# Attention with float32 probabilities and values in place of float16 high and low parts

## The reference, cut to what matters

```python
qg = split_heads(tokens @ Wqg, HEADS)      # 16 heads
kv = split_heads(tokens @ Wkv, HEADS)
queries, gates = qg[..., :16], qg[..., 16:]
keys, values = kv[..., :16], kv[..., 16:]  # values: 64 wide
queries, keys, values = l2norm(queries), l2norm(keys), l2norm(values)
sim = einsum('bhid,bhjd->bhij', queries, keys)
attn = square(relu(sim))
aggr = einsum('bhij,bhjd->bhid', attn, values)
out = tanh_norm(aggr) * tanh(silu(gates))
return out @ Wout
```

## Time and profile before

| | us |
|---|---|
| time, median of 2 runs | 3120.34 (3120.2 to 3120.49) |
| span of the profiled execution | 3118.2 |
| granted TensorE clock, mean | 0.976 |
| PE busy | 2774.7 (89%) |
| DVE busy | 2549.5 (82%) |
| ACT busy | 2288.4 (73%) |
| POOL busy | 888.1 (28%) |

### The profile page before, as it was taken

One profiled execution on the slowest core, in us unless ns is written; L12 is line 12 of the kernel. 1 busy time (PEld: TensorE's weight loads), 2 busy tenths in 40 slices (PEclk: granted clock), 3 DMA queues, 4 the chain that ended last, 5 costly groups with the idle time before them and its releaser, 6 DMA issues.

```text
span 3118.2 us, 54633 instructions
## 1 busy us (share of the span) xinstructions
PE 2774.7 (89%) x15168; PEld 1174.7 (38%) x15168; DVE 2549.5 (82%) x5207; ACT 2288.4 (73%) x4138; POOL 888.1 (28%) x683
## 2 busy tenths in 40 slices
PE   2898998989989899998989989899898998989999
PEld 1343343333433344333433334333343333434433
DVE  8987879778687887878878788786987879888796
ACT  3787767778677786877868678686776867778686
POOL 0314123141332413224132231412314123141332
PEclk8999999999999999999999999999999999999999
DMA  3000000000000000000000000000000000000000
GB/s 154 7 1 21 1 22 1 1 22 1 22 1 1 22 1 22 1 1 22 1 22 1 1 22 1 22 1 22 1 1 22 1 22 1 1 22 1 14 1 8
DMA packets 19501, 40.23 MB, mean 13 GB/s; under 512 B 1584, under 2 KB 9904, under 8 KB 18128
## 3 DMA queue, kind: packets, MB, share of 16 engines
q1 hardware_dynamic: 19152, 36.11, 3.4%
HBM read 27.72 MB, written 8.39 MB: 12 GB/s over the span
## 4 chain that ended last, share of the span: by engine, by line
PE 40%; DVE 35%; issue 14%; ACT 7%; DVEq 2%; POOL 1%; ACTq 0%; DMA 0%; SPq 0%; POOLq 0%
PE wk L1104 18%; DVE pl L589 10%; PE acc L1104 10%; DVE ph L585 7%; PE av L1177 5%; DVE wide L505 2%; PE sim L1163 2%; ACT ring L899 2%; PE wk L1186 2%; DVE hf L609 2%; DVE vn_t L418 1%; ACT ring L903 1%; ACT sg L909 1%; PE wk L1228 1%; DVE vn_y L420 1%
## 5 line engine op out<-in xcount | busy, mean ns | idle before, releaser
L1056 POOL TENSOR_TENSOR hl<-hf,hh 128x512 f16<-128x512 f32 x288 | 369.5, 1283 | 1645.8 <-ACT hh L915 1482.0
L589 DVE TENSOR_TENSOR pl<-ring,ph 128x512 f16<-128x512 f32 x1024 | 759.9, 782 | 0.0
L899 ACT ACTIVATE ring<-sim 128x512 f32<-128x512 f32 x1024 | 567.5, 603 | 250.3 <-PE sim L1163 176.6
L903 ACT ACTIVATE ring<-ring 128x512 f32<-128x512 f32 x1024 | 593.6, 640 | 0.0
L585 DVE CAST ph<-ring 128x512 f16<-128x512 f32 x1024 | 472.0, 497 | 83.0 <-ACT ring L903 54.3
L1177 PE MATMUL av<-ph,vh 128*64 128x512 f16 x1024 | 211.7, 410 | 42.5 <-DVE pl L589 42.4
L609 DVE SCALAR_TENSOR_TENSOR hf<-wk,up_routed,sg 128x512 f32<-128x512 f32 x256 | 191.6, 749 | 66.9 <-PE wk L1104 16.3
L909 ACT ACTIVATE sg<-wk,inv_m 128x512 f32<-128x512 f32 x288 | 199.6, 693 | 46.6 <-PE wk L1104 46.4
L1077 POOL TENSOR_TENSOR pl<-wide,ph 128x512 f16<-128x512 f32 x128 | 169.6, 1329 | 211.4 <-ACT ph L947 211.4
L641 DVE TENSOR_TENSOR gate_sb<-gate_sb,wk 128x512 f32<-128x512 f32 x128 | 87.8, 686 | 162.9 <-PE wk L1228 162.7
L1104 PE MATMUL acc<-hh,down_h 128*128 128x512 f16 x576 | 220.2, 382 | 0.0
(11 more groups left out here) (192 smaller groups left out, 5386.4 us busy)
## 6 DMA issues: line engine op xcount, KB each, us to landing
x_sb<-x SPq DMA_DIRECT2D x16, 512.0 KB, 4.9
y_sb<-x_t SPq DMA_DIRECT2D x16, 512.0 KB, 4.3
out_t<-y_sb SPq DMA_DIRECT2D x16, 512.0 KB, 3.2
raw_wa<-wa SPq DMA_DIRECT2D x1, 2560.0 KB, 9.1
raw_gate<-w_gate SPq DMA_DIRECT2D x1, 2304.0 KB, 14.2
raw_up<-w_up SPq DMA_DIRECT2D x1, 2304.0 KB, 19.3
raw_down<-w_down SPq DMA_DIRECT2D x1, 2304.0 KB, 24.3
raw_wo<-w_out SPq DMA_DIRECT2D x1, 1024.0 KB, 26.1
```

Source lines behind the costliest of these rows:

```text
L589: v.tensor_tensor(pl[:, n % NH_, :], ring[:, n % NR_, :], ph[:, n % NH_, :], ALU.subtract).then_inc(pl_done, 1)
L899: a(ring[:, n % NR_, :], sim[n % 2][:, :], ACT.Relu, scale=S_SCALE).then_inc(relu_done, 1)
L903: a(ring[:, n % NR_, :], ring[:, n % NR_, :], ACT.Square).then_inc(square_done, 1)
L1056: tt(hl[:, n % 2, :], hf[:, n % 2, :], hh[:, n % 2, :], ALU.subtract).then_inc(h_lo, 1)
```

## The change

The float16 parts of probabilities and values go. A probability stays in the `ring`, now of 8 slots; VectorE computes it as score (from PSUM) times relu (from the ring), and ScalarE's square, VectorE's cast and subtraction and the splits of v on ScalarE and GpSimd are gone. AV is one float32 matmul for each head, with the scaled values `v_raw` as weights and the ring slot as moving operand. As the score bank is now read by the square, S(s) waits for `square_done` where it waited for `relu_done`. `agg` gets a buffer of its own.

```diff
-        NR_, NH_ = 4, 2 * (LAG + 1)
+        NR_, NH_ = 8, 2
...
-        ph, pl = sb("ph", [P, NH_, T], F16), sb("pl", [P, NH_, T], F16)
+        ah, al = sb("ah", [P, NH_, T], F16), sb("al", [P, NH_, T], F16)
...
-        agg = wide
+        agg = sb("agg", [P, NP_, T])
...
-            def probs(b, n):
-                dve.wait_ge(square_done, upto(b, 2 * STEPS, n + 1))
-                dve.wait_ge(av_step, upto(b, STEPS, n // 2 - LAG))
...
-                v.tensor_copy(ph[:, n % NH_, :], ring[:, n % NR_, :]).then_inc(ph_done, 1)
-
-            def probs_lo(b, n):
...
-                v.tensor_tensor(pl[:, n % NH_, :], ring[:, n % NR_, :], ph[:, n % NH_, :],
-                                ALU.subtract).then_inc(pl_done, 1)
+            def square(b, n):
+                dve.wait_ge(relu_done, upto(b, 2 * STEPS, n + 1))
+                v.tensor_tensor(ring[:, n % NR_, :], sim[n % 2][:, :], ring[:, n % NR_, :],
+                                ALU.mult).then_inc(square_done, 1)
...
                     for n in (2 * s, 2 * s + 1):
-                        probs(b, n)
+                        square(b, n)
                     for kind, e in PLAN[s][len(lead):]:
                         expert_item(b, kind, e)
-                    for n in (2 * s, 2 * s + 1):
-                        probs_lo(b, n)
...
-            def split_hi_v(b, n):
...
             def relu(b, n):
                 act.wait_ge(sim_full, upto(b, 2 * STEPS, n + 1))
-                act.wait_ge(pl_done, upto(b, 2 * STEPS, n - NR_ + 1))
-                if n < NR_:
+                act.wait_ge(av_step, upto(b, STEPS, (n - NR_) // 2 + 1))
+                if n < NB:
                     act.wait_ge(qk_lo, upto(b, 2 * NB, 2 * NB))
-                a(ring[:, n % NR_, :], sim[n % 2][:, :], ACT.Relu, scale=S_SCALE).then_inc(relu_done, 1)
-
-            def square(b, n):
-                act.wait_ge(relu_done, upto(b, 2 * STEPS, n + 1))
-                a(ring[:, n % NR_, :], ring[:, n % NR_, :], ACT.Square).then_inc(square_done, 1)
+                a(ring[:, n % NR_, :], sim[n % 2][:, :], ACT.Relu, scale=S_SCALE * S_SCALE).then_inc(relu_done, 1)
...
-            def split_lo_v(b, n):
...
-                    pe.wait_ge(relu_done, upto(b, 2 * STEPS, n - 1))
+                    pe.wait_ge(square_done, upto(b, 2 * STEPS, n - 1))
...
-                pe.wait_ge(pl_done, upto(b, 2 * STEPS, 2 * s + 2))
+                pe.wait_ge(square_done, upto(b, 2 * STEPS, 2 * s + 2))
                 if pair == 0:
-                    pe.wait_ge(v_lo, upto(b, 2 * NB, 2 * (j + 1)))
+                    pe.wait_ge(vn_done, upto(b, 2 * NB, 2 * (j + 1)))
...
-                for i, (vv, pp) in enumerate(((vh, ph), (vl, ph), (vh, pl))):
-                    for half in range(2):
-                        h = 2 * pair + half
-                        ins = mm(av[64 * half:64 * half + 64, :], vv[:, j, h * DV:(h + 1) * DV],
-                                 pp[:, (2 * s + half) % NH_, :], start=(j == 0 and i == 0),
-                                 stop=(j == NB - 1 and i == 2))
+                for half in range(2):
+                    h = 2 * pair + half
+                    ins = mm(av[64 * half:64 * half + 64, :], v_raw[:, j, h * DV:(h + 1) * DV],
+                             ring[:, (2 * s + half) % NR_, :], start=(j == 0), stop=(j == NB - 1))
                 ins.then_inc(av_step, 1)
```

More of the change, by code:

```diff
@@ L209, in build_layer @@
         xh, xl = sb("xh", [P, KD, T], F16), sb("xl", [P, KD, T], F16)
-        NR_, NH_ = 4, 2 * (LAG + 1)
+        NR_, NH_ = 8, 2
         ring = sb("ring", [P, NR_, T])
-        qk_raw = ring[:, :, :]
+        qk_raw = ring[:, 0:NB, :]
         sq = sb("sq", [P, 2, T])
@@ L239, in build_layer @@
         y_sb = sb("y_sb", [P, KD, T])
-        ph, pl = sb("ph", [P, NH_, T], F16), sb("pl", [P, NH_, T], F16)
+        ah, al = sb("ah", [P, NH_, T], F16), sb("al", [P, NH_, T], F16)
         wide = sb("wide", [P, NP_, T])
         v_raw = wide[:, :, :].rearrange("p (k a) t -> p k (a t)", k=NB)
-        agg = wide
+        agg = sb("agg", [P, NP_, T])
         qst, kst = sb("qst", [P, 2, 2 * T], F16), sb("kst", [P, 2, 2 * T], F16)
         qt, kt = sb("qt", [P, NP_, T], F16), sb("kt", [P, NP_, T], F16)
-        vh, vl = sb("vh", [P, NB, H * DV], F16), sb("vl", [P, NB, H * DV], F16)
         sg = sb("sg", [P, 2, T])
@@ L250, in build_layer @@
         hh, hl = sb("hh", [P, 2, T], F16), sb("hl", [P, 2, T], F16)
-        ah, al = ph, pl
         vn_a, vn_y, vn_t = (sb(f"vn_{c}", [P, NB, H]) for c in "ayt")
@@ L270, in build_layer @@
         sim_full, relu_done, square_done = sem("sim_full"), sem("relu_done"), sem("square_done")
-        ph_done, pl_done, av_step = sem("ph_done"), sem("pl_done"), sem("av_step")
+        av_step = sem("av_step")
         agg_done, agg_sq_done = sem("agg_done"), sem("agg_sq_done")
@@ L280, in build_layer @@
         k_turned = sem("k_turned")
-        v_hi, v_lo = sem("v_hi"), sem("v_lo")
         score_done, route_step, ct_done = sem("score_done"), sem("route_step"), sem("ct_done")
@@ L577, in route @@
                 link.end()
-            def probs(b, n):
-                dve.wait_ge(square_done, upto(b, 2 * STEPS, n + 1))
-                dve.wait_ge(av_step, upto(b, STEPS, n // 2 - LAG))
-                if n < 4:
-                    dve.wait_ge(out_mm, upto(b, NP_, 0))
-                v.tensor_copy(ph[:, n % NH_, :], ring[:, n % NR_, :]).then_inc(ph_done, 1)
-            def probs_lo(b, n):
-                dve.wait_ge(ph_done, upto(b, 2 * STEPS, n + 1))
-                v.tensor_tensor(pl[:, n % NH_, :], ring[:, n % NR_, :], ph[:, n % NH_, :],
-                                ALU.subtract).then_inc(pl_done, 1)
+            def square(b, n):
+                dve.wait_ge(relu_done, upto(b, 2 * STEPS, n + 1))
+                v.tensor_tensor(ring[:, n % NR_, :], sim[n % 2][:, :], ring[:, n % NR_, :],
+                                ALU.mult).then_inc(square_done, 1)
             def weigh(b, e):
@@ L838, in raw @@
                 if n < NB:
-                    act.wait_ge(pl_done, upto(b, 2 * STEPS, 0))
+                    act.wait_ge(av_step, upto(b, STEPS, 0))
                     dst = qk_raw[:, n, :]
@@ L842, in raw @@
                     k, half = (n - NB) // 2, (n - NB) % 2
-                    act.wait_ge(a_hi, upto(b - 1, NP_, n - NB + 1))
-                    act.wait_ge(a_lo, upto(b - 1, NP_, n - NB + 1))
+                    act.wait_ge(av_step, upto(b, STEPS, 0))
                     dst = v_raw[:, k, half * T:half * T + T]
@@ L931, in take_heads @@
                 act.wait_ge(av_step, upto(b, STEPS, NB * (t + 1)))
-                act.wait_ge(v_lo, upto(b, 2 * NB, 2 * NB))
-                act.wait_ge(v_hi, upto(b, 2 * NB, 2 * NB))
+                act.wait_ge(a_hi, upto(b, NP_, 0))
+                act.wait_ge(a_lo, upto(b, NP_, 0))
                 a(agg[:, t, :], av[:, :], ACT.Copy).then_inc(agg_done, 1)
@@ L977, in whole @@
                 expert_item(b, *HEAD[3])
-                split_hi_v(b, 0)
-                split_hi_v(b, 1)
                 turned_k(b, 3)
@@ L985, in whole @@
                         relu(b, n)
-                    for n in (2 * s, 2 * s + 1):
-                        square(b, n)
                     for kind, e in PLAN[s]:
@@ L994, in whole @@
                             expert_item(b, kind, e)
-                    if s in (1, 2, 3):
-                        split_hi_v(b, 2 * s)
-                        split_hi_v(b, 1 + 2 * s)
                     if s % NB == LAG and s > NB:
@@ L1060, in body @@
                 hidden_lo(0)
-                for n in range(2):
-                    split_lo_v(b, n)
                 for s in range(STEPS):
@@ L1066, in body @@
                             hidden_lo(ORDER.index(e) - 1)
-                    if s in (1, 2, 3):
-                        split_lo_v(b, 2 * s)
-                        split_lo_v(b, 1 + 2 * s)
                 for kind, e in TAIL:
```

## The result

The changed kernel takes **3149.69 us** (median of 2 runs, 3148.45 to 3150.93) against 3120.34: a ratio of 1.0094, 95% interval 1.0065 to 1.0123. Under 2%, it counts as no change, to which the prediction gave 0.12. The profiled execution has a span of 3149.1 us, 30.9 more than that of before.

The account below looks back on a forecast made before the run. TensorE was taken to bound steps 10 to 30, waits for VectorE steps 2 to 9. Terms of +16.0 us a batch, 16 x 16.0 + 8.6 = 265, gave 3385 us, 8% slower; range 3160 to 3620.

Parts of the forecast that it names:

- the overlap of the halves: In AV: the two heads' fp32 matmuls overlap only staggered, three record times, 1.28 us, AV 1.41 in all.
- rival 3: In AV: halves overlap fully at two cycles a column, AV 0.98 us, total 3191 us; chance 0.08.
- +0.64: In each AV on TensorE: fp32 takes 1.41 us against 0.77, 0.64 us more.
- Steps 0 and 1: Loop start: scores wait for VectorE's products of v and squares; 9.5 us against 3.8, +5.7 a batch.
- Steps 2 to 9: Waits for VectorE vanish: 38.7 us falls to 26.2 + 8 x 0.64 = 31.3, -7.4 a batch.
- Half clock: Idle time at the loop's start may halve TensorE's clock: +2.4 us a batch, bounds 0 and 2.8.
- Steps 10 to 30: Packed steps where TensorE sets the pace: longer AVs add 21 x 0.64 = +13.4 us a batch.
- +1.3: Steps 9, 20 and 29, with u alone: scores wait for VectorE's chain, +1.3 us over the three.
- is worth nothing: Steps 10 to 30: less VectorE and ScalarE work saves no time, since TensorE sets the pace.
- Rival 2: Every step: the S, relu, square loop delays packed steps, 0.5 us in each of 22, about 3560 us; chance 0.08.
- The rest: Remainder of a batch outside steps 0 to 30: 3 x 0.64 - 1.3 = +0.6 us.
- the sum: Whole kernel: +16.0 us a middle batch, 16 x 16.0 + 8.6 for the last batch = 265 us more.

Follow-up runs that it names:

- the fastest one: Padded changed kernel with VectorE squaring the ring slot alone (relu times relu) and the scores waiting for relu; 3018.33 us, ratio 0.9675.
- the padded kernel: Changed kernel with 63 more TensorE instructions (waits on an already reached semaphore) ahead of the batch loop; 3131.68 us, ratio 1.0035.
- the moved kernel before: Kernel before the change with 128 more TensorE instructions ahead of the loop; 3155.22 us, ratio 1.0112.
- the halves apart: Changed kernel with AV's half 0 right behind S and half 1 left in place, for all but a batch's last two AVs; 3692.12 us.
- ScalarE without padding: Changed kernel with the square back on ScalarE, in place in the ring, scores waiting for relu, no added instructions; 3041.41 us, ratio 0.9756.
- one half alone: Changed kernel with the second head's value product made only for the first key block of each pair; 3135.01 us.

## Why the prediction was wrong

**The step that failed is the overlap of the halves**: "the second record of half 0 must follow the first, half 1's first can start beside it, its second follows. That is three record times". It is two: records start as half 0, half 1, half 0, half 1, 6 ns apart within a pair. A record does take about two f16 times, as I chose: 0.48 us lie between the two starts of one half, and two f16 matmuls of u take 2 x 0.218 = 0.44 (six in 1.31). I had carried the order in which the program lists matmuls over to the records that one matmul leaves, for which no row spoke; the f16 pairs of the earlier trace rows, side by side, were the nearest row and pointed to rival 3. Of the +0.64, 0.40 is missing: 0.40 x 512 = 205 of the 234 between forecast and measured span.

The rule of the Trainium skill that I set against rival 3 ("TensorE: Matmul & The Clock Gate", Part 3, a strict FIFO of matmuls) holds here for matmuls at most, not for records; whether the four are ordered so in the instructions or by the engine stays open. The four passes of the Trainium skill, "FP8 and Floating Point Precision", TensorE Precision Notes, fit: four f16 times of 0.218 are 0.87 of the 1.00 that one half takes.

**Steps 0 and 1**: place and mechanism right, +3.45 for +5.7. I made S(1) and S(2) wait for both squares of the step before. The code has each half of S wait for the square of its own half, so S(1) comes one square earlier (1457.77, while the second square still runs). Six products of v took 3.69, not 4.1: one after another they stand 0.60 apart, though each is recorded with 0.68. And where half clock falls before the loop, S(0) itself comes later and finds VectorE further on: the products of v begin 1.4 us ahead of it there, 0.2 in the batch shown, and the stretch takes 6.81 us against 7.97.

**Steps 2 to 9**: the waits for VectorE went as said. 26.2 + 8 x 0.24 = 28.1 was to be left; 28.95 is (a batch with full clock), and 0.5 of that is a wait for the square in step 2, which takes 3.66 us in the changed kernel and 3.16 in the fastest one. **Half clock** left the place behind step 8 and came to the start, as said, but costs less: 29.71 - 28.95 = 0.8 on the mean within these steps, for 2.4; in seven of the 13 batches it falls ahead of the loop, and these steps keep full clock.

**Steps 10 to 30**: 21 x 0.24 = 5.0, and +4.79 measured. The waits for the square are there, 2.0 us a batch in four steps (10, 21, 29, 30; +1.3 was forecast for three). I had written that VectorE's relief "is worth nothing" there. It was worth 2.3: three steps of before that took 3.99, 4.92 and 4.03 us take 3.52, 4.81 and 3.07 now, though each has an AV of 0.24 more. Rival 2 (a wait in every step) did not happen: outside these seven the packed steps grew by 0.24 alone.

**The rest**: -0.6 with the true price of AV, and the padded kernel shows 75.77 against 76.21, -0.4. The standstill puts 25.4 / 13 = 1.95 on top. That was in no term of the sum and in no rival. With AV at its true price the sum gives 16 x 3.2 + 8.6 = 60 us, against the measured 31. That it comes so near is in part luck: steps 0 and 1 were 2.3 us a batch too high and steps 10 to 30 1.5, and the standstill that was left out hides about half of this.

So the account of the time: float32 in TensorE costs 110 us, the wait for the square 113 (each taken out of the padded kernel by itself), the standstill 18 (15 where the wait is gone). That the first two add up, with neither hiding part of the other, was not tried. With the first alone of the three the kernel takes 3018.33, 102 less than before, so what leaves VectorE and ScalarE is worth more than float32 costs; with all three it is 29 more. Rival 3 had AV at 0.98 and 3191 us; it is 41 too high, though the standstill is not in it, because it took the same start and clock, and 26 us more for the u steps.

## What to carry to other kernels

Before an operation with no row of its own is priced, take the nearest row as it stands (here: two column halves run side by side) and give the departure from it the smaller chance. Where a chain of operations reads a PSUM tile, the program has to hold the next matmul into it until the last reader is done: reading the first operation's copy in SBUF instead took 113 us off, with the same engine and as many instructions. A small difference between two kernels of a loop may lie in where the loop's head falls: look for idle time without a releaser in the middle of a group of matmuls before explaining 1% by the edit.

## What the runs showed of the hardware that was not expected

- **Two float32 matmuls of 64 columns each** (128 rows, 512 columns of data) take 1.01 us side by side, one alone 1.00, and 2 x 1.01 if other matmuls stand between them.
- **The standstill ends with a packet of the instruction queue.** On the changed kernel's page this queue moves 2.49 MB in 152 packets, 16.4 KB each. In the traces, one such packet lands 6.2 to 7.7 us after each of the 13 jumps back to the loop's head, in kernels with and without a standstill. Four kernels stand still (the changed one, the moved kernel before, the halves apart, ScalarE without padding), and all their 52 standstills end 1.26 to 1.62 us after that packet has landed; in the round shown above it lands at 1621.25 and TensorE goes on at 1622.81. The earlier TensorE comes to the place, the longer it stands: 5.01 to 5.58 us behind the jump with the halves apart, 6.11 to 6.67 in the changed kernel, 6.97 to 7.24 with ScalarE.
- **The place is fixed in the program, not in the work.** Counted in the traces, 1961 TensorE instructions (weight loads, matmuls, register and semaphore instructions) stand ahead of the loop's head in the changed kernel and 2217 in the moved kernel before, 256 more: both stand still at the same matmul, 25 instructions further. With the halves apart it is 1972, 11 more, and the standstill comes 15 instructions behind the head, at nearly the same place of the program. With 2024 (padded), 2089 (before) and 1865 (one half alone) there is none. The Trainium skill, "Runtime: NRT & Kernel Launch", Instruction fetch mechanics, has instructions come in 16 KiB blocks of 256 and says that a taken branch out of the window waits for its block. The spacing of 256 and the size of the packets agree. The same section of the Trainium skill calls the crossing of a block mostly hidden; here the standstill held 0.86 to 4.15 us a round where it came soon behind a jump. That the packet holds the instructions that TensorE waits for is inferred from place and time; its contents are not in the trace.
- **Padding is no pure gain**: of the 25 us of standstill 9 went back to waits and half clock at the start of the loop, and the moved kernel before lost 35 to standstills of 23.7, partly by half clock behind them.
